# A routed product turned one unit ahead, with eight row buffers for its second part

## The chip, the cores and the metric

The kernel runs on one core of one Trainium2 chip. The metric is the device time of one execution in microseconds (us). Engine names are those of the profile: PE (TensorE matmuls), PEld (its weight loads), DVE (VectorE), ACT (ScalarE), POOL (GpSimd), SP (the queue that issues most DMAs).

## The reference

Input x is 64 sequences of 128 rows of 128, the context 64 x 120 rows. Four residual steps follow one another:

```
x = x + attention(layernorm(x) @ W0.T + b0, context, context)
x = x + shared_swiglu(n) + routed(n)             # n = layernorm(x)
x = x + attention(n Wq + bq, ctx Wk + bk, ctx Wv + bv)
x = x + trees(layernorm(x))                      # 8 decision trees of depth 7

def routed(x):                                   # 8 experts, H = 128, I = 256
    logits = x @ gate_w
    top_id, score = argmax(logits), sigmoid(max(logits))
    xs = x * score
    y = silu(xs @ rt_gate[e]) * (xs @ rt_up[e]) @ rt_down[e]   # e = top_id of the row
```

Each row goes through one expert only. The change touches the second step's routed part, and where the first steps of the second attention stand beside it.

## The kernel before, in words

Work is tiled by groups of G = 4 sequences (512 rows, NG = 16 groups). There are three stages in time.

*Phase A* (a_body, 19 rounds) computes the first attention, the shared expert and the logits of one group per round. Normalised rows are stored to rows2 in DRAM. DVE chooses each row's expert and its slot. POOL scales the rows by their score (scale) and scatters them with indirect DMAs, one per 128 rows, to x_sorted, a DRAM tensor in which every expert's rows fill whole tiles of 128 (scatter). This is done in two parts (halves) of 8 groups; the first part's 32 scatters lie in phase A, the second part's 32 follow it. The rows come back from rows2 into four buffers xs of one group each (load_rows, on SP); a buffer is loaded again when its four tiles have been scattered.

*The routed product* takes x_sorted in units of four tiles: 40 tiles a part, HR = 10 units, NR = 20 in both. For unit r SP loads it (r_load, two buffers xs_in), PE turns its tiles into PSUM bank 0 (r_turn), ACT copies them to xsT (r_evac_x), and PE multiplies them with the gate and up weights of each tile's expert, two tiles at a time, v = 0 and 1 (r_gate_up into banks 1, 2 and 3, 4). The weights were copied by DVE from WGU to w_now (r_weights), since the expert is known only at run time; experts_of reads it into registers. ACT takes silu (r_silu), DVE multiplies (r_mul), PE multiplies with the down weights (r_down, bank 6), and ACT copies the result to yo and stores it to y_sorted (r_evac_y). PE's order in r_body(r), line 1013: turn of unit r + 1, down of unit r - 1's second pair, first gate-up of unit r + 1, wait for the copy of y of unit r - 1, down of unit r's first pair, second gate-up of unit r + 1. All engines run in program order, so this order is set by hand. Units 1 to 8 are loops on PE and ACT, units 1 to 9 on DVE.

The second attention's steps for group 0, and some for group 1, are put by hand into late units, counted from FIRST_EARLY = HR + 2 = 12: c_rows3 (DVE adds routed rows and takes statistics), c_norm3, c_turn_x and c_scores (PE), c_xnT_evac and c_softmax (ACT), c_max_scores (DVE), c_turn_prob, c_pT_evac, c_values, c_rows4, c_norm4, c_turn_x4, c_x4_high, c_x4_low. DVE also splits the tree weights into a high and a low part there (split_trees_high, split_trees_low). POOL gathers the routed rows back by indirect DMA when the part's y is stored (gather).

*The trees* (phase_c, c_body) take one group per round of some 30 us; their first product is t_logits(0, 0), line 1125, behind a wait for the last copy of y at line 1123. The rest of the second attention runs inside these rounds.

The lines that matter: load_rows 441, SP's order after phase A 489 to 502, scale and scatter 530 to 546, POOL's order 572 to 576, ACT's r_body 730 to 755, PE's r_down 1004 and r_body 1013 to 1057, DVE's a_first_slots and a_pack (called at 1464 to 1468) and its units 1452 to 1498. These few lines set POOL's order for the second part:

```python
pool.wait_ge(scored, 2)
scale(HG)
pool.wait_ge(placed, 2)
for t in range(B0[1], B):
    scatter(t, 1, NG)        # calls scale(t // G + 1) at t % G == 2
```

## Time and profile before

| | |
|---|---|
| median of 3 runs | 853.05 us (853.01 to 855.39) |
| profiled execution | 849.45 us, its span 847.6 us |
| PE busy | 787.2 us, 93% of the span |
| PE weight loads | 633.5 us, 75% |
| DVE busy | 655.7 us, 77% |
| ACT busy | 541.6 us, 64% |
| POOL busy | 265.4 us, 31% |
| DMA | 55.88 MB, mean 66 GB/s |

The span runs from the first instruction to the last; the 1.8 us beside it lie around the program. Shares are means over stages that differ, so the rows below are read by stretch. In a timeline a number in brackets is the idle time of the engine before the instruction and, behind the arrow, what ended it; "issue" is time in which the profile shows no wait, and "remote" a release that it can't put to an instruction.

### The profile page before, as it was taken

To read this page: it belongs to the slowest core of one execution; us is meant where nothing else is said; L and a number is where in the kernel's file an instruction comes from. 1 tells how busy PE (TensorE), PEld (TensorE's weight loads), DVE (VectorE), ACT (ScalarE), POOL (GpSimd) and SP (SyncE) were. 2 spreads that over 40 slices of the span, in tenths; PEclk is the share of its full clock that TensorE was granted. 3 is DMA by queue.
4 is the path that set the end of the run, shared out by engine and by line. 5 is a ranking of instruction groups with operands and counts; after the bars stand their busy time and mean duration, and the time that the engine had idled before them with its cause. 6 is when DMAs were issued, how large, how long until landed. Compare 5 with 4: busy or idle time off the path is not lost.

```text
span 847.6 us, 15269 instructions
## 1 busy us (share of the span) xinstructions
PE 787.2 (93%) x4452; PEld 633.5 (75%) x4493; DVE 655.7 (77%) x1742; ACT 541.6 (64%) x948; POOL 265.4 (31%) x308
## 2 busy tenths in 40 slices
PE   5899998987878998999999999999999999999997
PEld 4788776776768898977777777777777777777775
DVE  5888889787844456768988887888888788888774
ACT  3577667565322334366877777777777777778765
POOL 2333222887287143112320321232132133111000
PEclk9999999999999999999999999999999999999999
DMA  6346784742334343100000000000000000000000
GB/s 170 89 137 191 194 221 130 202 130 85 87 108 149 95 116 91 51 26 13 26 23 4 25 25 0 25 25 19 6 25 25 0 25 25 11 14 14 14 1 25
DMA packets 91428, 55.88 MB, mean 66 GB/s; under 512 B 13439, under 2 KB 88055, under 8 KB 91255
## 3 DMA queue, kind: packets, MB, share of 16 engines
q1 hardware_dynamic: 75440, 41.29, 17.4%
q0 software_dynamic: 4096, 8.40, 3.5%
q10 hardware_dynamic: 11847, 5.64, 2.4%
q8 instruction: 23, 0.38, 0.2%
q14 instruction: 22, 0.18, 0.1%
HBM read 32.23 MB, written 23.07 MB: 65 GB/s over the span
## 4 chain that ended last, share of the span: by engine, by line
PE 41%; DVE 28%; issue 12%; ACT 12%; POOL 3%; another core or an unknown queue 2%; DVEq 1%; DMA 0%; ACTq 0%; POOLq 0%; SPq 0%
PE PS L823 7%; PE PS L808 6%; DVE sil_l L1522 4%; DVE dec L1506 3%; DVE xn_c L1149 3%; PE PS L1009 3%; PE PS L1068 3%; PE PS L1069 3%; PE PS L1070 3%; ACT sil L765 3%; DVE xn L1149 2%; PE PS L1090 2%; PE PS L1092 2%; PE PS L1091 2%; DVE st L1138 2%
## 5 line engine op out<-in xcount | busy, mean ns | idle before, releaser
L765 ACT ACTIVATE sil<-PS,b_in_c 128x512 f32<-128x512 f32 x256 | 162.3, 686 | 113.6 <-PE PS L1077 71.3
L1522 DVE TENSOR_TENSOR sil_l<-sil,sil_h 128x512 fp32r<-128x512 f32 x256 | 164.8, 685 | 44.7 <-ACT sil_h L773 44.3
L526 POOL TENSOR_TENSOR ve<-mv,eps 128x4 f32<-128x4 f32 x64 | 19.2, 300 | 450.2 <-DVE mv L1143 450.1
L773 ACT ACTIVATE sil_h<-sil 128x512 fp32r<-128x512 f32 x224 | 128.9, 631 | 0.0
L1090 PE MATMUL PS<-sil_h,wout_l 128*128 128x512 f32 x256 | 117.8, 460 | 1.6 <-DVE sil_l L1522 1.6
L1506 DVE TENSOR_SCALAR dec<-PS,b_in_c 128x512 bf16<-128x512 f32 x128 | 95.6, 747 | 26.1 <-PE PS L1070 24.3
L1068 PE MATMUL PS<-x4T_h,win_l 128*128 128x512 f32 x256 | 102.2, 399 | 1.6 <-ACT yo L725 0.7
L1092 PE MATMUL PS<-sil_h,wout_h 128*128 128x512 f32 x256 | 100.8, 394 | 0.0
L1091 PE MATMUL PS<-sil_l,wout_h 128*128 128x512 f32 x256 | 100.3, 392 | 0.0
L1069 PE MATMUL PS<-x4T_l,win_h 128*128 128x512 f32 x256 | 100.0, 390 | 0.0
L1070 PE MATMUL PS<-x4T_h,win_h 128*128 128x512 f32 x256 | 99.8, 390 | 0.0
L823 PE MATMUL PS<-xsT,w_now 128*128 128x128 f32 x640 | 81.4, 281 | 14.1 <-DVE ract L1442 6.9
L823 PEld LDWEIGHTS PS<-xsT,w_now 128*128 128x128 f32 x640 | 76.1, 195 | 16.3 <-issue 10.5
L584 POOL DMA_INDIRECT ys<-y_sorted,idx x64 | 69.8, 1090 | 28.1 <-issue 15.1
L528 POOL TENSOR_TENSOR rs<-ve,neg_half 128x4 f32<-128x4 f32 x64 | 70.6, 1103 | 5.0
L1090 PEld LDWEIGHTS PS<-sil_h,wout_l 128*128 128x128 f32 x256 | 48.3, 189 | 18.5 <-DVE sil_l L1522 6.4
L1209 DVE COPY w_now<-WGU 128x512 f32 x80 | 33.6, 461 | 36.7 <-PE PS L823 20.3
L1138 DVE BATCH_NORM_STATS2 st<-X 128x6 f32<-128x128 f32 (+1 forms) x256 | 55.5, 280 | 7.4 <-DMA X<-in_x 4.5
L1068 PEld LDWEIGHTS PS<-x4T_h,win_l 128*128 128x128 f32 x256 | 48.0, 188 | 17.3 <-issue 3.7
L1092 PEld LDWEIGHTS PS<-sil_h,wout_h 128*128 128x128 f32 x256 | 48.0, 188 | 11.2
L1070 PEld LDWEIGHTS PS<-x4T_h,win_h 128*128 128x128 f32 x256 | 48.0, 188 | 10.4
L1069 PEld LDWEIGHTS PS<-x4T_l,win_h 128*128 128x128 f32 x256 | 48.1, 188 | 9.4
(169 smaller groups left out, 1549.6 us busy)
## 6 DMA issues: line engine op xcount, KB each, us to landing
x_sorted<-zeros SPq DMA_DIRECT2D x4, 1280.0 KB, 6.8
xs_in<-x_sorted SPq DMA_DIRECT2D x20, 256.0 KB
y_sorted<-yo ACTq DMA_DIRECT2D x20, 256.0 KB
X<-in_x SPq DMA_DIRECT2D x16, 256.0 KB
rows<-xn SPq DMA_DIRECT2D x16, 256.0 KB
out<-res SPq DMA_DIRECT2D x16, 256.0 KB
ctxT<-in_ctx_t SPq DMA_DIRECT2D x16, 240.0 KB
ctx_rows<-in_ctx_kv SPq DMA_DIRECT2D x16, 240.0 KB
```

The lines of the kernel that those rows point to most:

```text
L765: act.activation(tile(sil[p % 2], c, W), bank(2 * (p % 2) + c), ACT.Silu, bias=b_in_c[:, 2 * p + c:2 * p + c + 1]).then_inc(t_silu, 1)
L773: act.activation(tile(sil_h[p % 2], c, W), tile(sil[p % 2], c, W), ACT.Copy).then_inc(t_hi, 1)
L823: i = pe.matmul(tile(bank(1 + 2 * v + t), n), tile(w_now[v], 2 * FC * t + n), tile(xsT[u], 2 * v + t), start=True, stop=True)
L1068: pe.matmul(dst, lo, x4T_h, start=True, stop=False, skip_group_check=True)
L1069: pe.matmul(dst, hi, x4T_l, start=False, stop=False, skip_group_check=True)
L1070: i = pe.matmul(dst, hi, x4T_h, start=False, stop=True, skip_group_check=True)
L1090: pe.matmul(bank(4), lo, act_h, start=(p == 0 and c == 0), stop=False)
L1091: pe.matmul(bank(4), hi, act_l, start=False, stop=False)
L1092: pe.matmul(bank(4), hi, act_h, start=False, stop=(p == TREES - 1 and c == 1)).then_inc(t_out, 1)
L1138: i = dve.bn_stats(st[:, s, j, :], cols(X, g * W + j * P, P))
L1506: dve.tensor_scalar(dec[p % 2], bank(2 * (p % 2)), b_in_c[:, 2 * p:2 * p + 1], 0.0, ALU.add, ALU.is_gt).then_inc(t_dec, 1)
L1522: dve.tensor_tensor(tile(sil_l[p % 2], c, W), tile(sil[p % 2], c, W), tile(sil_h[p % 2], c, W).bitcast(F32), ALU.subtract).then_inc(t_lo, 1)
```

## The change

- The turn of unit r + 2 is done in PE's r_body(r) after the first gate-up of unit r + 1; before, r_body(r) began with the turn of unit r + 1. Unit 1's turn moves into phase A.
- Row groups 12 to 15 get buffers of their own (late_rows, in the room of the shared expert's weights and rows), so the second part has eight. SP loads groups 10 to 15 at once after phase A, and no longer between units.
- POOL scales groups 8 to 11, all before the first scatter of the second part; ACT scales groups 12 to 15, four activations each, in units 1 to 4 between the copy of xsT and the second silu.
- Unit 9 and unit 19 have three tiles in place of four (39 tiles a part, since eight experts can leave at most seven partly filled tiles beside 32 full ones); y_sorted is one tile shorter.
- Steps of the second attention and the weight splits stand elsewhere in the late units; x4_low of group 0 and norm3, turn and copy of group 1 stand behind the last unit. ACT's loop over units is written out; DVE's loop ends at unit 7.
- The wait for the last copy of y stands behind the first tree product.

The diff, without the changed call signatures (r_weights, r_mul, r_silu and r_down take (r, v) for q) and the narrowing of their tiles to pair_tiles(r, v):

```diff
         xs = cut.two("xsa", W)
+        cut = Cut(TREE_W // 2, TREE_W)
+        late_rows = [cut.take(f"late_rows{i}", W) for i in range(XB)]
...
+        def rows_of(k):
+
+            return late_rows[k - HG - XB] if k >= HG + XB else xs[k % XB]
...
+        def near_end(r):
+
+            return isinstance(r, int) and r >= NR - 2
+
+        def pair_tiles(r, v):
+
+            return 1 if v and isinstance(r, int) and r in (HR - 1, NR - 1) else 2
+
+        def unit_tiles(r):
+
+            return 2 + pair_tiles(r, 1)
...
-                if i:
+                if k >= HG + XB:
+                    sp.wait_ge(a_g_ps, NG)
+                elif i:
                     sp.wait_ge(scattered[v], 16 * G * i)
                 sp.wait_ge(a_rows, 16 * (k + 1))
-                sp.dma_start(by_tile(xs[v]), rows2[k * G:(k + 1) * G, :, :].rearrange("b s d -> s b d")
-                             ).then_inc(k_in[v], 16)
+                sp.dma_start(by_tile(rows_of(k)), rows2[k * G:(k + 1) * G, :, :].rearrange("b s d -> s b d")
+                             ).then_inc(late_in[v] if k >= HG + XB else k_in[v], 16)
...
-            for k in range(HG + 2, HG + XB):
+            for k in range(HG + 2, NG):
                 load_rows(k)
             for r in range(HR - 2):
                 r_next(r, r % 2, 0)
-                if r > 2 and HG + XB + r - 3 < NG:
-                    load_rows(HG + XB + r - 3)
...
-                v = (t // G) % XB
-                if t % G == 2 and t // G + 1 < end:
-                    scale(t // G + 1)
-                pool.wait_ge(k_scaled, t // G + 1)
+                k = t // G
+                v = k % XB
+                if t % G == 2 and k + 1 < end:
+                    scale(k + 1)
+                if k < HG + XB:
+                    pool.wait_ge(k_scaled, k + 1)
+                else:
+                    pool.wait_ge(k_late, k - HG - XB + 1)
                 pool.sem_inc(pool_passed, 1)
                 pool.indirect_dma_start(x_sorted[h], bass.IndirectOffsetOnAxis(ap=POS[:, t:t + 1], axis=0),
-                                        tile(xs[v], t % G), None).then_inc(scattered[v], 16)
+                                        tile(rows_of(k), t % G), None).then_inc(scattered[v], 16)
...
-            scale(HG)
+            for k in range(HG, HG + XB):
+                scale(k)
             pool.wait_ge(placed, 2)
             for t in range(B0[1], B):
-                scatter(t, 1, NG)
+                scatter(t, 1, HG)
...
+            def scale(k):
+                act.wait_ge(late_in[k % XB], 16)
+                rows = rows_of(k)
+                for j in range(G):
+                    i = act.activation(tile(rows, j), tile(rows, j), ACT.Identity,
+                                       scale=SCORE[:, k * G + j:k * G + j + 1])
+                i.then_inc(k_late, 1)
...
-                r_silu(2 * r, 0)
-                if not last_unit(r):
+                r_silu(r, 0)
+                if r < NR - 1:
                     r_evac_x(r + 1, 1 - u)
-                if isinstance(r, int) and r == FIRST_EARLY + 3:
+                if 1 <= r <= XB:
+                    scale(HG + XB + r - 1)
+                if r == FIRST_EARLY + 3:
                     c_xnT_evac(0)
-                r_silu(2 * r + 1, 1)
-                if not first(r):
-                    r_evac_y(r - 1, 1 - u, stores, 1 if isinstance(r, int) and r > HR else 0)
-
-            r_body(0, 0, None)
-            with act.Fori(0, HR // 2 - 1) as i:
-                r_body(2 * i + 1, 1, i)
-                r_body(2 * i + 2, 0, i)
-            for r in range(HR - 1, NR):
+                if r == FIRST_EARLY + 4:
+                    c_softmax(0)
+                if r == FIRST_EARLY + 5:
+                    c_pT_evac(0)
+                if r == FIRST_EARLY + 7:
+                    c_x4_high(0)
+                r_silu(r, 1)
+                if r:
+                    r_evac_y(r - 1, 1 - u, stores, 1 if r > HR else 0)
+
+            for r in range(NR):
                 r_body(r, r % 2, (r - 1) // 2)
-                if r == FIRST_EARLY + 3:
-                    c_softmax(0)
-                if r == FIRST_EARLY + 4:
-                    c_pT_evac(0)
-                if r == FIRST_EARLY + 6:
-                    c_x4_high(0)
-                if r == FIRST_EARLY + 7:
-                    c_xnT_evac(1)
             r_evac_y(NR - 1, 1, NR // 2 - 1, 1)
+            c_xnT_evac(1)
...
                     r_gate_up(0, 0, 0, 0)
+                    r_turn(1, 1)
...
@@ -1016,25 +1044,24 @@
                 q = 2 * r
                 if not end:
                     coming = experts_of(pe, r + 1)
-                    r_turn(r + 1, 1 - u)
                 if not first(r):
-                    r_down(q - 1, 1, was)
+                    r_down(r - 1, 1, was)
                 if not end:
                     r_gate_up(q + 2, 0, r + 1, 1 - u)
+                    if not near_end(r):
+                        r_turn(r + 2, u)
                 if now is None:
                     now = experts_of(pe, r)
                 if isinstance(r, int):
                     if r == FIRST_EARLY + 3:
                         c_scores(0)
-                    if r == FIRST_EARLY + 4:
-                        c_turn_prob(0)
-                    if r == FIRST_EARLY + 6:
+                    if r == FIRST_EARLY + 5:
+                        c_values(0)
+                    if r == FIRST_EARLY + 7:
                         c_turn_x4(0)
-                    if r == FIRST_EARLY + 7:
-                        c_turn_x(1)
                 if not first(r):
                     pe.wait_ge(r_y, r)
-                r_down(q, 0, now)
+                r_down(r, 0, now)
                 if end:
                     return now
                 r_gate_up(q + 3, 1, r + 1, 1 - u)
...
                 if r == FIRST_EARLY + 2:
                     c_turn_x(0)
                 if r == FIRST_EARLY + 4:
-                    c_values(0)
+                    c_turn_prob(0)
             now = r_body(NR - 1, 1, now, coming, end=True)
-            r_down(2 * NR - 1, 1, now)
+            r_down(NR - 1, 1, now)
+            c_turn_x(1)
...
-            pe.wait_ge(r_y, NR)
             pe.wait_ge(tree_split, 2)
             t_logits(0, 0)
+            pe.wait_ge(r_y, NR)
             phase_c(pe, c_body)
...
-            with dve.Fori(1, HR) as r:
+            with dve.Fori(1, HR - 2) as r:
                 coming = r_first(r)
                 r_second(r, coming)
-            for r in range(HR, NR - 1):
+            for r in range(HR - 2, NR - 1):
                 coming = r_first(r)
                 if r == FIRST_EARLY + 1:
                     c_rows3(0)
-                if r == FIRST_EARLY + 3:
-                    c_max_scores(0)
-                if r == FIRST_EARLY + 5:
-                    c_rows4(0)
+                if r == FIRST_EARLY + 2:
+                    c_norm3(0)
                 if r == FIRST_EARLY + 6:
-                    c_rows3(1)
+                    c_norm4(0)
                 r_second(r, coming)
                 if r == HR + 1:
                     split_trees_high()
+                if r == FIRST_EARLY:
+                    split_trees_low(win_l, win_f, win_h)
                 if r == FIRST_EARLY + 2:
-                    c_norm3(0)
-                if r == FIRST_EARLY + 1:
-                    split_trees_low(win_l, win_f, win_h)
+                    split_trees_low(wout_l, wout_f, wout_h)
+                if r == FIRST_EARLY + 3:
+                    c_max_scores(0)
                 if r == FIRST_EARLY + 4:
-                    split_trees_low(wout_l, wout_f, wout_h)
+                    c_rows3(1)
                 if r == FIRST_EARLY + 5:
-                    c_norm4(0)
-                if r == FIRST_EARLY + 6:
-                    c_x4_low(0)
-                    c_norm3(1)
-            r_mul(2 * NR - 2, 0)
-            r_mul(2 * NR - 1, 1)
+                    c_rows4(0)
+            r_mul(NR - 1, 0)
+            r_mul(NR - 1, 1)
+            c_x4_low(0)
+            c_norm3(1)
```

## Rows read from the trace of the kernel before

**Rows 1.** The page's first line: span and number of instructions.
```profile
span 847.6 us, 15269 instructions
```

**Rows 2.** Stretches (start:end, length): busy us (x instructions) by engine, clock, DMA.
```profile
225.95:241.95 16.00, 11.54 (x98) 10.90 (x97) 12.05 (x26) 3.86 (x7) 9.33 (x10) 1.00 0.25 74
241.95:282.09 40.14, 31.91 (x262) 29.84 (x261) 15.88 (x29) 11.30 (x20) 29.61 (x30) 1.00 0.44 135
282.09:317.61 35.52, 35.52 (x313) 35.22 (x313) 19.59 (x40) 13.04 (x24) 9.35 (x10) 1.00 0.37 102
317.61:330.60 12.99, 12.35 (x110) 12.16 (x109) 10.59 (x26) 4.35 (x8) 7.86 (x8) 1.00 0.36 105
330.60:365.83 35.23, 31.74 (x263) 30.99 (x261) 22.57 (x59) 15.72 (x26) 2.91 (x4) 0.95 0.19 54
365.83:847.60 481.77, 469.53 (x2232) 353.50 (x2272) 395.53 (x929) 356.97 (x585) 108.69 (x123) 1.00 0.06 17
294.18:300.04 5.86, 5.86 (x55) 5.86 (x53) 2.90 (x6) 2.17 (x4) 0.00 (x0) 1.00 0.31 89
```

**Rows 3.** Timeline of PE in body 9: turn, down, gate-up, down.
```profile
294.18 0.60 PE L808 MATMUL PS<-WA,xs_in 128*128 128x128 f32 x4
294.62 1.06 PE L1009 MATMUL PS<-WD,ract 128*128 x8
295.51 2.01 PE L823 MATMUL PS<-xsT,w_now 128*128 128x128 f32 x16
297.36 1.06 PE L1009 MATMUL PS<-WD,ract 128*128 x8
```

**Rows 4.** Timelines of DVE, POOL and PE where the second part is placed.
```profile
213.79 0.20 DVE L1380 TENSOR_TENSOR expert_f<-expert_f,c_rout 128x40 f32<-128x40 f32 x1
...
223.95 0.94 DVE L1357 CAST tiles_f<-tiles_i 128x8 f32<-128x8 int32 x1
...
232.42 1.72 DVE L1380 TENSOR_TENSOR expert_f<-expert_f,c_rout 128x40 f32<-128x40 f32 x1
...
223.83 1.04 POOL L534 TENSOR_TENSOR xsa<-xsa,SCORE 128x512 f32<-128x512 f32 x1 [9.51 <-ACT SCORE L633]
...
237.38 2.05 PE L823 MATMUL PS<-xsT,w_now 128*128 128x128 f32 x16 [2.53 <-DVE ract L1442]
```

**Rows 5.** Timelines in bodies 3 and 4: late copies, and what waits for them.
```profile
249.31 0.66 PE L808 MATMUL PS<-WA,xs_in 128*128 128x128 f32 x4
...
252.64 0.60 ACT L629 ACTIVATE xsT<-PS 128x512 f32<-128x512 f32 x1 [5.03 <-remote]
...
253.46 2.05 PE L823 MATMUL PS<-xsT,w_now 128*128 128x128 f32 x16 [2.60 <-issue]
...
261.13 2.05 PE L823 MATMUL PS<-xsT,w_now 128*128 128x128 f32 x16 [1.61 <-ACT xsT L629]
...
263.31 0.69 DVE L1442 TENSOR_TENSOR ract<-sg,PS 128x512 f32<-128x512 f32 x1 [2.64 <-remote]
...
264.02 1.15 PE L1009 MATMUL PS<-WD,ract 128*128 x8 [0.85 <-issue]
```

**Rows 6.** Timeline of POOL: first and last of the second part's 32 scatters.
```profile
230.72 1.01 POOL L545 DMA_INDIRECT x_sorted<-xsa,POS  x1 [5.86 <-DVE POS L1370]
...
279.07 0.96 POOL L545 DMA_INDIRECT x_sorted<-xsb,POS  x1 [0.30 <-issue]
```

**Rows 7.** Body 15: DVE's maximum, PE's next gate-up, and the stretch behind.
```profile
334.87 0.66 DVE L1403 TENSOR_REDUCE nmax<-PS 128x4 f32<-128x480 f32 x1 [3.48 <-PE PS L977]
...
337.63 3.51 PE L823 MATMUL PS<-xsT,w_now 128*128 128x128 f32 x16 [1.90 <-DVE ract L1442]
...
338.00:342.00 4.00, 4.00 (x23) 4.00 (x23) 1.44 (x4) 0.99 (x3) 0.00 (x0) 0.59 0.00 0
```

**Rows 8.** The last unit: DVE's norm3 of group 1, PE's first tree product.
```profile
359.97 1.11 DVE L1149 TENSOR_SCALAR xn_c<-X,mv,rs 128x128 f32<-128x128 f32 x4
...
365.83 0.50 PE L1068 MATMUL PS<-x4T_h,win_l 128*128 128x512 f32 x1 [0.69 <-ACT yo L725]
```

More of the change, by code:

```diff
@@ L85, in program @@
     x_sorted = [nc.dram_tensor(f"x_sorted{h}", (HTILES[h] * P, P), F32, kind="Internal").ap() for h in range(HALVES)]
-    y_sorted = [nc.dram_tensor(f"y_sorted{h}", (HTILES[h] * P, P), F32, kind="Internal").ap() for h in range(HALVES)]
+    y_sorted = [nc.dram_tensor(f"y_sorted{h}", ((HTILES[h] - 1) * P, P), F32, kind="Internal").ap() for h in range(HALVES)]
     rows2 = nc.dram_tensor("rows2", (B, P, P), F32, kind="Internal").ap()
@@ L324, in last @@
             return isinstance(g, int) and g >= NG - n
-        def last_unit(r):
-            return isinstance(r, int) and r == NR - 1
+        def near_end(r):
[4 more added lines that the diff above has]
+            return 2 + pair_tiles(r, 1)
         DVE_TREE = 1
@@ L714, in c_x4_high, with r_silu @@
                 act.activation(x4T_h, bank(7), ACT.Copy).then_inc(c_x4h, 1)
[L717 to L720 removed]
+            def r_silu(r, v):
+                n = pair_tiles(r, v)
+                act.wait_ge(r_gu_ps, 2 * r + v + 1)
+                pair = by_tile(PS[:, 512 * (1 + 2 * v):512 * (1 + 2 * v + n)], 512)
+                act.activation(by_tile(sg[v][:, 0:n * FI], FI), pair[:, :, 0:FI], ACT.Silu).then_inc(r_sg, 1)
             def r_evac_y(r, u, stores, h):
@@ L820, in r_gate_up @@
                     pe.wait_ge(r_act, q - 1)
-                for t in range(2):
+                for t in range(pair_tiles(r, v)):
                     for n in range(2 * FC):
@@ L1002, in _, with r_down @@
             pe.wait_ge(a_rows, 16 * NG)
-            def r_down(q, v, experts):
-                pe.wait_ge(r_act, q + 1)
-                for t in range(2):
+            def r_down(r, v, experts):
+                pe.wait_ge(r_act, 2 * r + v + 1)
+                for t in range(pair_tiles(r, v)):
                     for c in range(FC):
@@ L1202, in take_logits, with r_weights @@
                 dve.tensor_tensor(dst, dst, src[:, :, 0:n, E:2 * E], ALU.add).then_inc(a_lg, 1)
-            def r_weights(q, v, experts):
-                if not below(q, 2):
-                    dve.wait_ge(r_gu_ps, q - 1)
-                for t in range(2):
+            def r_weights(r, v, experts):
+                if not below(r, 1):
+                    dve.wait_ge(r_gu_ps, 2 * r + v - 1)
+                for t in range(pair_tiles(r, v)):
                     i = dve.tensor_copy(tile(w_now[v], t, 2 * FI),
@@ L1241, in a_body @@
                     a_choose(4)
[L1242 removed]
+                    r_weights(0, 1, experts_of(dve, 0))
                 if route == "pack":
```

41 lines of the change are left out of this document (20 added, 21 removed).

## The prediction

> **What bounds the kernel now.** I read the span first [rows 1], then busy time by stretches cut at the starts of units [rows 2], and inside those stretches each engine's timeline for what ended its idle time. "Body r" is PE's r_body(r); it starts with the turn of unit r+1. The kernel has three stages: phase A up to 226 us, the routed product from 226 to 366 us, and the trees from 365.83 us to the end. The change works on the second. The trees take 481.8 us, PE busy in 469.5 of them [rows 2]; nothing in their loop is edited, so I carry that stretch over unchanged.
>
> An undisturbed body is PE-bound: 5.86 us with PE busy for all of it, DVE for 2.90 and ACT for 2.17 [rows 2]. It is turn 0.44, down 0.89, gate-up 1.85, down 0.89 (starts 294.18, 294.62, 295.51, 297.36 [rows 3]), and the remaining 5.86 - 4.07 = 1.79 is the second gate-up. Against 5.86 each, the stretches of rows 2 overrun as follows:
> - bodies 0 and 1: 16.00 - 11.72 = 4.3 us
> - bodies 2 to 6: 40.14 - 29.30 = 10.8 us; this is where the second part's scatters run [rows 6]
> - bodies 7 to 12: 35.52 - 35.16 = 0.4 us
> - bodies 13 and 14: 12.99 - 11.72 - 0.44 (attention's turn) = 0.8 us
> - body 15 to the first tree product: 35.23 us, worked out below
>
> So the stage has some 20 us that isn't PE work. The question is which of it the change reaches.
>
> **Part 1, the end of the stage (moved attention steps, tile 39 of unit 19, tree logits ahead of the last wait).** Before, DVE takes attention's row maximum in the middle of body 15, idle 3.48 us until the scores are there; the weights of the next gate-up queue behind it, and PE idles 1.90 us [rows 7]. The gate-up after that takes 3.51 us instead of 1.85. After the change the maximum stands behind DVE's second half, which is done when silu is; DVE's 1.3 us of maximum and shift then end before body 15 does, and the weights (0.76 us) are ready 0.9 us into body 16. ScalarE's exp with its two table loads (1.28 us each) stands in ScalarE's body 16 ahead of silu, whose product PE wants only a body later. I find no new PE wait in bodies 15 to 18. The tightest place is the first weights copy of DVE's unit 18, behind attended rows and statistics: on my schedule it ends 0.1 us before PE wants it.
>
> PE's sum from body 15: body 15 with scores (eight matmuls, as a down, 0.89) 6.75; body 16 5.86; turn of prob 0.44; body 17 with values 6.75; body 18 without a turn and with a one-tile second gate-up 5.86 - 0.44 - 0.90 = 4.52; then down 0.89, attention's turn 0.44, downs 0.89 + 0.45, turn 0.44. That is 27.4. The tail gains waits: turn, x4 high on ScalarE (0.60, the length of the evacuation in rows 5), silu, y's evacuation, then the last downs; and on DVE product, x4 low and norm3 (1.11 [rows 8]) before the last turn. I put these at 1.6 + 0.3 = 1.9 us. Total 29.3 against 35.2: **5.9 us saved**. Today's tail also idles 0.69 us before the first tree product, for the last y [rows 8]; that wait moves behind the product.
>
> **Part 2, bodies 13 and 14.** DVE's routed rows and statistics (some 2.2 us) and the 2.3 us split of win no longer fall into one body. DVE's own 2.9 us plus 2.3 fits in 5.86. **0.8 us saved.**
>
> **Part 3, 39 tiles in unit 9.** One tile less of gate-up (half of 1.79) and of down (half of 0.89) in a PE-bound body: **1.3 us saved.** Turning still does four tiles.
>
> **Part 4, the turn a unit ahead, in bodies 2 to 6.** Here I see a lag that I can't explain. The turn at 249.31 should be over by 250, yet ScalarE's copy of it starts at 252.64, and PE's next gate-up at 253.46, 2.60 us idle. The same form gives 1.61 us at 261.13 [rows 5] and a third, smaller one 0.6, 4.8 us together. In the new order the turn is followed by attention steps, down, a gate-up and the next body's down before its result is needed: 0.89 + 1.79 + 0.89 = 3.6 us, less 0.6 of copying, is 3.0 us of cover against 0.3 now. That covers all three. A second lag, from a down to y's evacuation and the next down, cost 0.85 at 264.02 [rows 5] and 0.2 at 270.9; its cover grows by the turn's 0.44, so 0.6 back. **5.4 us saved**, if it is a lag of the signal. If the array itself stands still, looking ahead gives back nothing; these are my two ends, 0 and 5.4, and I take 5.4, because PE's records run on during the lag: it starts the gate-up at 261.13 while the down before it is signalled only at 263.3, when DVE's product that waits for it starts [rows 5]. The Trainium skill, page "SBUF — State Buffer", section "SBUF: two separate sides", says that DMA traffic can't slow an engine's SBUF access; that speaks for a lag over a stalled array, and the trace, where DMA is busiest just there, can't yet tell.
>
> **Part 5, scaling and buffers.** POOL scatters 32 tiles from 230.72 to 280.0 [rows 6], with seven scales between. A scale is 1.05 us and a scatter has a pitch of 1.27, so without scales 32 x 1.27 = 40.6 us: the end comes near 272. Nothing that sets the end waits for it: load 10 was free to start at 282 and its turn came at 294. Moving it early costs at the front. Scales 9, 10 and 11 now run back to back behind scale 8 at 223.83, next to DVE's routing chain, which is what holds PE to 237.38 (2.53 idle) [rows 4]. The 0.17 us cast L1357 took 0.94 beside scale 8, and L1380 took 1.72 beside the scale that stands at 233.0 against 0.20 alone [rows 4]. So the chain loses up to 3 x 1.05 = 3.2 us, and gains 1.5 from the scale that leaves its place there; bounds -1.5 and +3.2. Most of the chain's steps are much shorter than the POOL work around them, so I take +1.5, which gives a sum of **0**. The Trainium skill, page "SBUF — State Buffer", section "Who interferes with whom", calls this an exclusive lock, held for a whole instruction; L1357 and L1380 agree. By that rule alone each added scale can hold the chain once, the upper bound.
>
> ScalarE's four scales (four 128x128 each; between 0.6 us, one 128x512 [rows 5], and 2.4, four such) fall in bodies 1 to 4, where ScalarE is idle 3.7 us of 5.86 and about 2 of it at that place. I take 1.0 and cost it at nothing. SP's four more row loads (1 MB) go ahead of load 2, which then lands 3 to 5 us later, still before its turn near 229.7.
>
> **Sum.** 5.9 + 0.8 + 1.3 + 5.4 + 0 = 13.4 us. The profiled execution took 849.45 us (span 847.6 and 1.8 around it), so 836.0 for one profiled like it; the median of the runs shown is 3.6 us above it, and 853.05 - 13.4 = **839.6 us**.
>
> **Rivals.**
> - *The lag stays (0.25).* PE really stands still in bodies 2 to 6, and the scatters are as many as before. Only 8.0 us come back: 845.0. For it: the overrun is only where scatters run. Against: PE's records run on.
> - *The lag goes altogether (0.12).* It comes from rows, scales and scatters together; rows and scales leave. 10.8 instead of 5.4 us back: 834.2.
> - *DVE's chain gets longer (0.12).* Each of the three scales holds it once: +3.2, without the gain: 842.8.
> - *PE's clock (0.05).* After today's 1.90 us idle PE ran 338 to 342 at a granted clock of 0.59, which is the level of 1.2 GHz for most of it; the gate-up at 337.63 took 3.51 us [rows 7]. The new tail has a 1.6 us idle of its own, so the fall may come back at the first trees: 1.7 us lost, 841.3.
> - *It does nothing measurable (0.05).* That needs the end of the stage to be refilled by DVE: rows 4 ahead of unit 18's weights late by several us. About 852.
> - *Slower (0.04).* ScalarE stands in order: its wait for late row group 12 is ahead of unit 1's second silu, near 237 us. The load leaves SP near 218. Each us beyond 237 delays all engines; the change is slower from a landing at about 251 us on, and at 256 costs 5 us net: 858. Against it: the DMA engines are a quarter busy from 226 on [rows 2].
>
> **How the numbers follow.** The forecast has 0.37. The range takes in the four cases from 834.2 to 845.0 with about 1 us for the spread of runs: 833.5 to 847. A measurement here tells 0.3% (2.6 us) from no change. Faster: the forecast and the first four rivals, 0.91, less some doubt on steps I haven't seen: 0.89. Same 0.06, slower 0.05.
>
> **What would show it.** Part 1: PE without a wait above 0.5 us from the start of body 15 to the last unit, no fall of its clock near 338, and 29 us to the first tree product. Part 4: copies of the turn may still start late, but no gate-up idles for them; wrong if bodies 2 to 6 still sum to 40 us. Part 5: last scatter near 272; unit 2's first gate-up starts within 1.5 us of 237.4. The trees must again take 482 us. The prediction fails if ScalarE or DVE waits in bodies 1 to 4 for rows, or if the overrun in bodies 2 to 6 doesn't move.

## The result, and the profile after

The change made the kernel slower on the chip of its first measurement: a median of 862.64 us (861.47 to 862.72) against 853.03 us, a ratio of 1.0124 with a 95% interval of 1.0084 to 1.0164. The prediction was 839.6 us, with a range of 833.5 to 847.0: wrong in sign. On another chip, below, the same two kernels come out at a ratio of 0.993, some 6 us saved, where the forecast's sum without Part 4 is 8.0.

The profiled execution after has a span of 859.7 us [rows 1: 847.6]. Its stretches, cut where those of [rows 2] are (start of body 2, of body 7, of body 15, first tree product); the first start is worked out, 238.58 of unit 2's gate-up below plus 1.85 + 0.44 + 0.89 + 1.79; columns as in [rows 2]:

```profile
span 859.7 us, 15178 instructions
243.55:300.91 57.36, 38.45 (x284) 36.99 (x285) 17.42 (x36) 16.95 (x37) 22.99 (x24) 0.79 0.28 83
300.91:347.37 46.46, 46.46 (x416) 46.46 (x417) 31.55 (x65) 17.81 (x32) 17.51 (x17) 1.00 0.37 107
347.37:377.89 30.52, 27.68 (x246) 27.29 (x245) 19.48 (x56) 14.01 (x24) 2.47 (x4) 1.00 0.19 53
377.89:859.70 481.81, 470.14 (x2235) 353.30 (x2273) 395.52 (x929) 357.87 (x587) 108.56 (x123) 1.00 0.06 17
```

Where the 12.06 us (377.89 - 365.83) went:

| stretch | before | after | difference |
|---|---|---|---|
| start of body 2 (after has one turn more ahead of it, 0.4) | 241.95 | 243.55 | +1.6 |
| bodies 2 to 6 | 40.14 | 57.36 | +17.2 |
| bodies 7 to 14 | 48.51 | 46.46 | -2.05 |
| body 15 to the first tree product | 35.23 | 30.52 | -4.7 |
| trees | 481.77 | 481.81 | 0 |

So the later stretches did about what was forecast, and one stretch, bodies 2 to 6, lost more than all of it. PE there, body 1 to body 2 and again in body 3:

```profile
235.84 1.95 PE L850 MATMUL PS<-xsT,w_now 128*128 128x128 f32 x16
237.62 1.12 PE L1037 MATMUL PS<-WD,ract 128*128 x8
238.58 1.95 PE L850 MATMUL PS<-xsT,w_now 128*128 128x128 f32 x16
240.36 0.27 PE L835 MATMUL PS<-WA,xs_in 128*128 128x128 f32 x1
241.53 0.38 PE L835 MATMUL PS<-WA,xs_in 128*128 128x128 f32 x2 [0.89 <-issue]
...
258.59 2.07 PE L1037 MATMUL PS<-WD,ract 128*128 x8 [15.29 <-issue]
...
273.20 0.48 PE L850 MATMUL PS<-xsT,w_now 128*128 128x128 f32 x2 [0.45 <-issue]
274.61 0.50 PE L850 MATMUL PS<-xsT,w_now 128*128 128x128 f32 x3 [0.93 <-issue]
```

PE's records stop for 15.29 us. Just before this hole, and again from 273 us on, its groups of four and sixteen matmuls come broken into ones, twos and threes with idle time between them. Behind the hole the matmuls run at half their speed (2.07 us for a down that takes 1.06): the granted clock is 0.50, the level of 1.2 GHz, from 246 to 262 us. The signals for the same matmuls, in ACT and DVE:

```profile
235.23 1.26 ACT L651 ACTIVATE late_rows<-late_rows,SCORE 128x128 f32<-128x128 f32 x4
247.24 0.60 ACT L749 ACTIVATE sg<-PS 128x512 f32<-128x512 f32 x1 [10.74 <-remote]
257.80 0.60 ACT L755 ACTIVATE yo<-PS 128x512 f32<-128x512 f32 x1 [9.96 <-remote]
...
261.47 0.60 ACT L749 ACTIVATE sg<-PS 128x512 f32<-128x512 f32 x1 [3.08 <-remote]
...
247.46 0.94 DVE L1237 COPY w_now<-WGU 128x512 f32 x2 [9.61 <-remote]
```

The silu at 247.24 wants the gate-up recorded at 235.84, and the copy of y at 257.80 the down recorded at 237.62: 9.5 and 19 us after their ends (237.79 and 238.74). The silu at 261.47 wants the gate-up recorded at 238.58, 21 us after its end (240.53). So what PE's records call done is signalled far later. This trace doesn't tell whether the work itself or only its signal was late; a_gather below says something on it. The record of 258.59 stands behind such a signal: PE's program waits there for the copy of y, 257.80 + 0.60 = 258.40, and that copy waits for PE's own down. POOL beside it, 20 scatters without a pause from 232.93 on, and then:

```profile
257.10 0.96 POOL L564 DMA_INDIRECT x_sorted<-late_rows,POS  x1 [0.30 <-issue]
264.52 0.96 POOL L564 DMA_INDIRECT x_sorted<-late_rows,POS  x1 [6.46 <-ACT late_rows L651]
...
280.69 0.96 POOL L564 DMA_INDIRECT x_sorted<-late_rows,POS  x1 [6.25 <-ACT late_rows L651]
```

The signal that lets PE go on comes at 257.80, inside the last scatter of POOL's burst (257.10 to 258.06), and not before. POOL stops only because ScalarE's next scale, in ScalarE's order behind copies and silus that wait for PE, hasn't been done. Then POOL starts the next burst, of eight, at 264.52, and PE is slowed in it again: from unit 4's turn (266.01) to unit 6's (285.61) it takes 19.6 us for two bodies. The scatters end at 285.65, not near 272.

### The profile page after: what moved, and what is told of

The parts are those of the page before. It is cut to its first block, busy times and chain, and to the rows that moved or that the text cites. A ratio compares the mean times of both kernels' runs of the same rounds, so it can differ in the third digit from the quotient of the medians.

```text
span 859.7 us, 15178 instructions
## 1 busy us (share of the span) xinstructions
PE 789.1 (92%) x4436; PEld 636.0 (74%) x4477; DVE 653.4 (76%) x1740; ACT 546.5 (64%) x964; POOL 259.5 (30%) x304
## 3 DMA queue, kind: packets, MB, share of 16 engines
q1 hardware_dynamic: 75440, 41.29, 17.2%
## 4 chain that ended last, share of the span: by engine, by line
PE 45%; DVE 27%; issue 14%; ACT 10%; POOL 3%; DVEq 1%; another core or an unknown queue 1%; DMA 0%; ACTq 0%; POOLq 0%; SPq 0%
PE PS L850 8%; PE PS L835 6%; PE PS L1037 4%; DVE sil_l L1551 4%; DVE dec L1535 3%; DVE xn_c L1177 3%; PE PS L1096 3%; PE PS L1098 3%; PE PS L1097 3%; ACT sil L792 3%; PE PS L1118 2%; DVE xn L1177 2%; PE PS L1120 2%; PE PS L1119 2%; PE PS L858 2%
## 5 line engine op out<-in xcount | busy, mean ns | idle before, releaser
L850 PEld LDWEIGHTS PS<-xsT,w_now 128*128 128x128 f32 x632 | 78.5, 202 | 8.5 <-issue 7.8
L604 POOL DMA_INDIRECT ys<-y_sorted,idx x64 | 71.9, 1123 | 27.9 <-issue 15.1
L749 ACT ACTIVATE sg<-PS 128x512 f32<-128x512 f32 (+1 forms) x40 | 23.5, 586 | 76.6 <-PE PS L850 60.2
L1237 DVE COPY w_now<-WGU 128x512 f32 x78 | 30.6, 432 | 48.3 <-PE PS L850 28.4
L1037 PE MATMUL PS<-WD,ract 128*128 x312 | 44.5, 288 | 18.0 <-issue 15.3
```

The source lines that it names most:

```text
L850: i = pe.matmul(tile(bank(1 + 2 * v + t), n), tile(w_now[v], 2 * FC * t + n), tile(xsT[u], 2 * v + t), start=True, stop=True)
L1037: i = pe.matmul(tile(bank(6), 2 * v + t), tile(ract[v], FC * t + c), cols(WD, experts[2 * v + t] * (FC * P) + c * P, P), start=(c == 0), s ...
```

## The experiments

The theory (theory 1 in what was expected): POOL's indirect DMAs, issued without a pause, hold PE's array or its signals; before, POOL's scale after every fourth scatter let PE go, and the change took these scales away. Rivals: the hold comes from the scatters' writes and the DMA traffic; from PE's register reads of the experts; from the new PE order; or from the row loads that SP issues at once, with POOL's pauses having no part. The yardstick is the time from unit 3's turn to unit 8's, five bodies (T3 to T8): 29.3 us by the undisturbed body of [rows 3], 40.14 before and 57.2 after. Kernels of one chip share their runs of the kernel before.

### Chip 8 (before 847.76 us)

**a_poolscale**: the change, with POOL scaling every group between scatters, as before.

```diff
-                if k < HG + XB:
-                    pool.wait_ge(k_scaled, k + 1)
-                else:
-                    pool.wait_ge(k_late, k - HG - XB + 1)
+                pool.wait_ge(k_scaled, k + 1)
...
-            for k in range(HG, HG + XB):
-                scale(k)
+            scale(HG)
             pool.wait_ge(placed, 2)
             for t in range(B0[1], B):
-                scatter(t, 1, HG)
+                scatter(t, 1, NG)
...
-                if 1 <= r <= XB:
-                    scale(HG + XB + r - 1)
```

> The changed kernel with one part undone: POOL scales all groups itself, one scale of 1.05 us after every fourth scatter, as before; ScalarE's four scales and POOL's three scales ahead of the first scatter go; eight buffers and all else stay. Theory 1 (PE stands still while POOL issues scatters without a pause; each pause lets it go on): the 15.3 us gap of PE goes, the bodies from unit 2's first gate-up to body 7 take about 45 us again in place of 62, and the time falls by 17 to 20 us, to about 844. Rival 2 (the new order on PE, with the turn behind the gate-up, makes the stall): it stays, about 861. Rival 3 (the four more row loads at 218 us make it): it stays too, and so would a gap in a kernel that only has those.

Measured: 843.1 us, ratio 0.9927 (0.9897 to 0.9958); T3 to T8 34.07 us. One part undone, and there is a gain of 0.7% where the first chip had a loss of 1.2%; the change as it is wasn't run on chip 8, but a_gather and a_static below, which differ from it elsewhere, take 860.84 and 858.89 us here. What is left of the hold shows its form. POOL's scales, ACT's and DVE's first work after them:

```profile
251.10 1.05 POOL L552 TENSOR_TENSOR late_rows<-late_rows,SCORE 128x512 f32<-128x512 f32 x1
257.22 1.05 POOL L552 TENSOR_TENSOR late_rows<-late_rows,SCORE 128x512 f32<-128x512 f32 x1
263.47 1.05 POOL L552 TENSOR_TENSOR late_rows<-late_rows,SCORE 128x512 f32<-128x512 f32 x1
...
251.23 0.60 ACT L748 ACTIVATE sg<-PS 128x512 f32<-128x512 f32 x1 [4.07 <-remote]
258.12 0.60 ACT L748 ACTIVATE sg<-PS 128x512 f32<-128x512 f32 x1 [3.92 <-remote]
264.36 0.60 ACT L748 ACTIVATE sg<-PS 128x512 f32<-128x512 f32 x1 [3.63 <-remote]
...
279.49 0.69 DVE L1468 TENSOR_TENSOR ract<-sg,PS 128x512 f32<-128x512 f32 x1 [4.78 <-remote]
```

Each late signal comes within or at the end of a scale; the last burst has six scatters (270.93 to 278.27) and no scale behind it, and there the signal comes 1.2 us after its end. That last burst costs more behind the yardstick: from unit 8's turn (273.09) to unit 9's (283.57) it takes 10.48 us, 4.7 above a body of 5.80. The theory holds; PE's new order and SP's row loads are still in this kernel, so these two rivals fall as causes of the large hold.

**b_eight**: the kernel before, with the eight buffers and the new scaling alone.

```diff
-            scale(HG)
+            for k in range(HG, HG + XB):
+                scale(k)
             pool.wait_ge(placed, 2)
             for t in range(B0[1], B):
-                scatter(t, 1, NG)
+                scatter(t, 1, HG)
...
+                if isinstance(r, int) and 1 <= r <= XB:
+                    scale(HG + XB + r - 1)      # on ScalarE
```

> The kernel before with one part of the change alone: eight row buffers, groups 8 to 11 scaled by POOL ahead of the first scatter, groups 12 to 15 by ScalarE in units 1 to 4 (its loop over units written out for that), and all row loads after phase A. PE's order, the attention steps and 40 tiles stay. Theory 1 (scatters without a pause): PE gets a gap of 10 us and more here too, the time rises by 15 to 20 us, to about 870. Rival 2 (PE's new order): the time stays within 2 us of before, or 3 above it for DVE's chain beside POOL's scales.

Measured: 866.53 us, ratio 1.0201 (1.0157 to 1.0244). The one part alone makes the loss, in PE's old order too. Its two holes lie ahead of unit 3's turn (262.62), so the yardstick misses them: T3 to T8 is 37.2 us, and unit 2's turn to unit 8's 62.9 us, against 48.8 in the kernel before on the first chip.

```profile
245.50 3.64 PE L841 MATMUL PS<-xsT,w_now 128*128 128x128 f32 x16 [7.10 <-issue]
257.41 2.07 PE L1027 MATMUL PS<-WD,ract 128*128 x8 [8.27 <-ACT yo L745]
```

**a_gather**: the change, with the second part's indirect DMAs reading from x_sorted into the row buffers in place of writing, so that part's rows don't reach x_sorted.

```diff
-                pool.indirect_dma_start(x_sorted[h], bass.IndirectOffsetOnAxis(ap=POS[:, t:t + 1], axis=0),
-                                        tile(rows_of(k), t % G), None)
+                pool.indirect_dma_start(tile(rows_of(k), t % G), None, x_sorted[h],
+                                        bass.IndirectOffsetOnAxis(ap=POS[:, t:t + 1], axis=0))
```

> The changed kernel with the second part's 32 scatters turned round: the same 32 indirect DMAs of 128 rows at the same places of POOL's program, but from x_sorted to the row buffers. The second part of the routed product is thus computed from zeros and its result isn't the reference's. If POOL's issuing of indirect DMAs without pause holds PE, the gap of about 15 us stays. If it is the direction, rows read from SBUF and written to DRAM, PE has no gap above 2 us in bodies 1 to 6, and the time is near 842.

Measured, one execution: 860.84 us, T3 to T8 55.9 us. The direction doesn't matter. Two silus of this run say something on the signals:

```profile
262.70 0.60 ACT L753 ACTIVATE sg<-PS 128x512 f32<-128x512 f32 x1 [15.57 <-remote]
...
264.84 0.59 ACT L753 ACTIVATE sg<-PS 128x512 f32<-128x512 f32 x1
```

The first wants the gate-up recorded from 239.46 to 241.51. Between that gate-up and the next silu's, PE does a turn, a down and a gate-up, 28 matmuls: 3.1 us at 0.11 us each, and some 6 us at the granted clock of 0.50 here. The two silus are 2.14 us apart. So PE had done part of the 28 before the first silu started: the signal came later than the work.

**a_static**: the change, with PE using experts 0 to 3 for every unit's down product in place of the ones it reads.

```diff
+            if eng is nc.tensor:
+                return [0, 1, 2, 3]
             word = eng.value_load(
```

> The changed kernel, but PE reads no expert numbers from SBUF and always takes the down weights of experts 0 to 3 (its result isn't the reference's); matmuls, waits and signals are as many. If PE's own register reads, or addresses that are known only at run time, are what waits behind POOL's scatters, the gap goes and the time is near 842. If the array or PE's signals are held, the gap of about 15 us stays, and the time is within 2 us of the changed kernel.

Measured, one execution: 858.89 us, T3 to T8 54.8 us. The rival of the register reads falls. And in this kernel the hold is seen matmul by matmul:

```profile
247.32 0.37 PE L852 MATMUL PS<-xsT,w_now 128*128 128x128 f32 x1 [1.16 <-issue]
248.01 0.37 PE L852 MATMUL PS<-xsT,w_now 128*128 128x128 f32 x1 [0.33 <-issue]
...
255.73 0.37 PE L1039 MATMUL PS<-WD,ract 128*128 128x128 f32 x1 [1.51 <-issue]
256.43 0.37 PE L1039 MATMUL PS<-WD,ract 128*128 128x128 f32 x1 [0.33 <-issue]
257.13 0.58 PE L1039 MATMUL PS<-WD,ract 128*128 128x128 f32 x1 [0.33 <-issue]
259.93 0.37 PE L1039 MATMUL PS<-WD,ract 128*128 128x128 f32 x1 [2.22 <-issue]
```

Starts are 0.70 us apart, or 1.4, 2.1 and 2.8; at full speed they are 0.11 apart (16 in 1.79). At most one or two matmuls start in 0.70 us until 262.03, 3.2 us after POOL's burst ended (257.86 + 0.96 = 258.82; its next scatter is at 264.64). So the array or what feeds it is slowed as well, and not only a signal late.

### Chip 1 (before 840.02 us)

**a_half**: the change, with POOL scaling two tiles after every second scatter (all groups on POOL).

```diff
+                if h and t % G == 2 and k + 1 < end:
+                    scale_half(k + 1, 0)
+                if h and t % G == 0 and k > HG:
+                    scale_half(k, 1)
```

> The changed kernel, but POOL scales all groups of the second part itself, two tiles (128x256, some 0.55 us) after every two scatters, so that no more than two scatters follow each other without a pause, except the last four; eight buffers and PE's new order stay. Theory 1 (PE slows down more the longer POOL issues scatters without a pause; from the third or fourth on it all but stands): bodies 1 to 6 lose nearly nothing, PE's stretch from unit 2's first gate-up to body 7 is near 38 us, the time 4 to 6 us below the one with pauses after every four, about 838. Rival (each scatter costs PE a fixed time, whatever stands between): as with pauses after every four, about 843.

Measured: 838.98 us, ratio 0.9987 (0.9978 to 0.9997); T3 to T8 29.7 us.

**a_land4**: the change, with POOL waiting after every fourth scatter until the four have landed.

```diff
                                         tile(rows_of(k), t % G), None).then_inc(scattered[v], 16)
+                if h and t % G == G - 1:
+                    pool.wait_ge(scattered[v], 16 * G * (k // XB + 1))
```

> The changed kernel with one wait added: after each fourth scatter of the second part POOL waits until the four have landed, and does no other work in the pause. Scaling stays as the change has it. If only POOL's pause matters, whatever fills it, PE's 15 us gap goes and the time is near 845. If the scales themselves (an operation that holds DVE's port) are what lets PE go on, the gap stays, near 860.

Measured, one execution: 846.65 us; T3 to T8 29.8 us.

**a_pooldma** and **a_spdma**: the change, with the second part's rows stored by plain DMAs in row order in place of by expert (so x_sorted's second part holds other rows), issued by POOL and by SP.

```diff
-                pool.indirect_dma_start(x_sorted[h], ..., tile(rows_of(k), t % G), None)
+                pool.dma_start(x_sorted[h][(t - B0[1]) * P:(t - B0[1] + 1) * P, :], tile(rows_of(k), t % G))
```

> The changed kernel with the second part's 32 scatters as plain DMAs of the same 128 rows from POOL, to rows in order, no list of addresses (the routed result isn't the reference's). If any DMA whose descriptors POOL writes holds PE, the gap stays, about 860. If it is the indirect form alone, the gap goes, about 842.

> The changed kernel with the second part's 32 scatters as plain DMAs issued by SP, four after each load of a unit (the routed result isn't the reference's); POOL issues nothing there, the bytes and descriptors moved are the same. If POOL's writing of descriptors holds PE, PE has no gap above 1 us in bodies 1 to 7 beyond the front, and the time is 835 to 840. If the DMA traffic itself holds PE, gaps of several us remain.

Measured, one execution each: 833.08 and 833.71 us, neither with a hold.

But nothing was held on this chip in any of the four, and before itself took 840 us, not 848 to 853. So these four say nothing on the hold yet. They do show a limit that the hold had covered. In a_half the scatters end at 280.06, and in a_land4 near 288; unit 10's load wants them all, and PE arrives at it earlier now:

```profile
285.15 1.11 PE L848 MATMUL PS<-WA,xs_in 128*128 128x128 f32 x4 [4.69 <-DMA xs_in<-x_sorted]
...
292.77 1.11 PE L837 MATMUL PS<-WA,xs_in 128*128 128x128 f32 x4 [10.57 <-DMA xs_in<-x_sorted]
```

### Chip 9 (before 840.47 us): is it the chip?

**before2** and **after2** are the two kernels unchanged, **a_poolscale2** and **a_half2** repeat a_poolscale and a_half.

> The kernel before, unchanged, to have its profile from the chip of this series, since its time was 853, 848 and 840 us in three series. If chips differ in how much POOL's scatters hold PE, bodies 2 to 6 take another time here than the 40.1 us of the first profile (29.3 if not held at all), and phase A and the trees take the same. If chips differ otherwise, these move too.

> The changed kernel, unchanged, beside the others on one chip. It should again have a gap on PE behind the fifth or so of the scatters without a pause; on a chip where the kernel before is at 840 us, the ratio to before is then above the 1.012 of the first series if the long burst holds PE everywhere, and below it if such a chip hardly knows the hold.

> Scales on POOL after every fourth scatter, all else as changed: again 0.7% below before (0.990 to 0.996). On a chip with little hold it gains only what doesn't hang on scatters, some 8 us of the sum, 1%, if load 10 doesn't come late.

> Half scales on POOL after every second scatter: PE isn't held in bodies 2 to 6 (cadence 5.8 to 6.1 us), but PE waits for load 10, since the last scatter is issued only near 280 us; between 0.990 and 1.000 of before, the same as with pauses after every four within 2 us.

Measured: before2 841.04 us (one execution), after2 834.1, ratio **0.993** (0.9908 to 0.9953), a_poolscale2 835.42, ratio 0.9942 (0.9921 to 0.9964), a_half2 839.03, ratio 0.9988 (0.9974 to 1.0002). Bodies 2 to 6 of before2 and of after2 (here to the worked-out end of body 6; body 7's down starts at 273.04):

```profile
244.05:274.62 30.57, 30.54 (x263) 29.39 (x261) 15.35 (x30) 10.86 (x20) 25.07 (x26) 1.00 0.55 162
...
242.81:272.72 29.91, 29.50 (x262) 29.10 (x260) 14.95 (x30) 13.71 (x28) 22.90 (x24) 1.00 0.44 130
```

The same kernels, with more bytes per us than on the first chip (162 GB/s against 135 in [rows 2]), and no hold in either; after2 was expected to have one. The hold goes with the chip. But the runs of one chip were made together and no numbered chip was visited twice, so nothing tells the chip from something else that may have changed with it. Here the change is faster, and its scaling part is worth something: after2's scatters end at 274.1 and unit 10's turn, at 281.61, waits for nothing, while a_poolscale2 waits 0.79 us and a_half2 4.94 us there.

### Chip 6 (before 853.28 us)

**a_pooldma2** and **a_land4b** repeat a_pooldma and a_land4.

> The changed kernel with plain DMAs from POOL for the second part's 32 scatters (routed result isn't the reference's), once more, since the first time the kernel before was at 840 us and such a chip hardly knows the hold. If this series has the kernel before at 847 us or more: the gap of 10 us and more on PE stays if any DMA from POOL makes it, about 860; it goes, about 840, if it needs the indirect form. With before at 840 us it tells nothing new: about 833.

> The changed kernel with POOL waiting after each fourth scatter until the four have landed, once more. With before at 847 us or more: PE is held 1 to 2 us in each burst of four as in the kernel before, and then waits some 5 to 10 us for load 10, about 850, if a pause in which POOL does nothing is as good as one with a scale; a gap of 10 us inside the scatters if it isn't. With before at 840 us: about 846, the wait for load 10 alone.

Measured, one execution each: a_pooldma2 834.46 us, T3 to T8 29.8 us: no hold from 32 plain DMAs with as many bytes on the same queue, the first 24 of them back to back from 234.10 to 247.41. That this chip does hold is seen in a_mix below. So the rival of the traffic falls; it takes the indirect kind. Their issue is shorter too, eight in 4.57 us, and a long issue by itself can't be told from the indirect kind by this. a_land4b took 845.56 us, T3 to T8 33.1 us, then 4.49 us for unit 10's load; against 57.2 in the change as it is. Its pauses are idle:

```profile
234.10 4.57 POOL L565 DMA_DIRECT2D x_sorted<-xsa  x8 [4.05 <-DVE POS L1402]
...
239.86 0.96 POOL L564 DMA_INDIRECT x_sorted<-xsa,POS  x1 [2.11 <-DMA x_sorted<-xsa,POS]
246.71 0.96 POOL L564 DMA_INDIRECT x_sorted<-xsb,POS  x1 [2.10 <-DMA x_sorted<-xsa,POS]
```

The first line is a_pooldma2, the others a_land4b. ScalarE's scales and the front are here as in the change, so the pause is what frees PE, whether POOL computes in it or not. In this pause the four DMAs also land; a pause with DMAs in flight was tried only with a scale in it.

**a_mix**: the change, with groups 9 to 11 scaled by POOL between scatters, and a memset of 128x32 ahead of every second one of the last sixteen.

```diff
-                if t % G == 2 and k + 1 < end:
+                if t % G == 2 and k + 1 < min(end, HG + XB):
                     scale(k + 1)
+                if h and t % G in (0, 2) and k >= HG + XB:
+                    pool.memset(tile(pad, (t - (HG + XB) * G) // 2, 32), 0.0)
```

> The changed kernel with scales 9, 10 and 11 back on POOL between scatters, and for groups 12 to 15, which ScalarE scales, a memset of 128x32 on POOL ahead of every second scatter as a pause. With before at 840 us: as fast as the change without its longer front, 1 to 2 us below it, 0.990 to 0.993 of before. With before at 847 us or more: if a pause of some 0.3 us is enough, 0.985 to 0.990; if it must be as long as a scale, PE gets gaps of several us in the last 16 scatters, 1.00 to 1.01.

Measured: 857.49 us, ratio 1.0054 (1.0029 to 1.008); T3 to T8 53.2 us. The memset fits into the 0.30 us between two scatters, their pitch doesn't grow, and PE's records have a hole of 14.59 us where the scales end; the copy of y that ends it starts at 272.11, 3.1 us after the burst's last scatter (268.97). A scale of 1.05 us is enough of a pause, a memset of 0.14 to 0.28 us inside the gap is not.

## Why the prediction was wrong, step by step

**Part 4, the overrun of bodies 2 to 6: the step that failed.** I saw the 10.8 us, saw that they lay only where scatters ran, gave a stalled array a chance of 0.25, and then let that case cost nothing more than a saving missed. My two ends were 0 and 5.4 us saved. The lower end was not an end: with a stalled array, the change edits what stalls it. "The scatters are as many as before" was true, and the pauses between them, which Part 5 took away, were what bounded the hold. The measured value is -17.2 us, where +5.4 was forecast. By the runs, b_eight and a_poolscale, the scaling part alone accounts for the loss. The argument for a lag ("PE's records run on") was half the matter: signals do come late, by up to 21 us after the records, but the matmuls are slowed too (0.70 us and more between starts in a_static), and both come from the same bursts, which looking ahead doesn't shorten. The trace before had a sign that the length of a burst counts, and I didn't use it. Its last six scatters, 272.69 to 280.03, have no scale among or behind them, and at their end a gate-up comes broken into eleven, four and one, with 1.9 us idle:

```profile
277.88 1.39 PE L823 MATMUL PS<-xsT,w_now 128*128 128x128 f32 x11
279.88 0.62 PE L823 MATMUL PS<-xsT,w_now 128*128 128x128 f32 x4 [0.61 <-issue]
281.31 0.27 PE L823 MATMUL PS<-xsT,w_now 128*128 128x128 f32 x1 [0.81 <-issue]
282.09 0.65 PE L808 MATMUL PS<-WA,xs_in 128*128 128x128 f32 x4 [0.51 <-issue]
```

The sentence of the Trainium skill, page "SBUF — State Buffer", section "SBUF: two separate sides", on DMA traffic that I set against it didn't decide the matter either: plain traffic holds nothing (a_pooldma2), as it says. The Trainium skill says in that section, of the SBUF ports, that PE and ACT "never wait on anyone". PE does wait beside POOL's indirect DMAs here, and no run shows whether it is at a port; whoever reads the sentence as "nothing on POOL can slow PE" is set right by the measurement. Whether looking ahead gives anything where nothing is held: on chip 9 bodies 2 to 6 took 30.57 us before, so there was at most 1.3 to win. Whether it gives anything where PE is held isn't shown: no pair of runs on one such chip differs in PE's order alone.

**Part 5, the front.** Three added scales held DVE's chain once each:

```profile
223.79 0.93 DVE L1385 CAST tiles_f<-tiles_i 128x8 f32<-128x8 int32 x1
224.76 0.97 DVE L1386 TENSOR_TENSOR_SCAN tile_end<-c_rout,tiles_f 128x8 f32<-128x8 f32 x1
225.76 0.96 DVE L1387 TENSOR_TENSOR first_slot<-tile_end,tiles_f 128x8 f32<-128x8 f32 x1
226.75 0.97 DVE L1388 TENSOR_SCALAR first_slot<-first_slot 128x8 f32<-128x8 f32 x1
...
234.63 0.20 DVE L1408 TENSOR_TENSOR expert_f<-expert_f,c_rout 128x40 f32<-128x40 f32 x1
```

The first took 0.94 already [rows 4]; the next three are short steps stretched to a scale's length, 0.8 us each, and the fifth gives back 1.5 (1.72 in [rows 4]). That is +0.9 for the sum of 0 that I took, and unit 2's first gate-up starts at 238.58, 1.2 later than 237.38. I argued from short chain steps beside long POOL work; the point is that a short step too is held until the scale ends, and four scales back to back catch four steps. The rule of an exclusive lock in the Trainium skill, page "SBUF — State Buffer", section "Who interferes with whom", gave the upper end, and the count of held steps agrees with it. ScalarE's scales took 1.26 us, not 1.0. That these scales should stand behind work that waits for PE, and so set POOL's pace through PE's own delay, was in no step; it is what closes the loop at 258 and 274 us.

**"Nothing that sets the end waits for the scatters."** True for PE's old pace, with unit 10's turn at 294 [rows 3]. In after2 that turn is at 281.61, and the scatters' end at 274.1 is then needed (a_half2 waits 4.94 us for an end at 280).

**Part 3, 39 tiles: mis-sized.** I took half a gate-up and half a down, 1.3 us. Only the down is narrower:

```profile
310.82 1.95 PE L850 MATMUL PS<-xsT,w_now 128*128 128x128 f32 x16
...
318.40 0.61 PE L1037 MATMUL PS<-WD,ract 128*128 x4
```

The second down of unit 9, at 318.40, has four matmuls. Its second gate-up, at 310.82, still has sixteen, since body 8 issues it inside PE's loop, where the unit is a register and pair_tiles gives 2. The body takes 5.35 instead of 5.80: 0.45 us.

**Part 2 and bodies 7 to 14.** 2.05 us came back against 2.1 forecast (parts 2 and 3), but from other places: 0.45 from the tile, 8 x 0.06 = 0.5 because an undisturbed body is 5.80 and not 5.86 (the first gate-up 1.79 instead of 1.85, no longer right behind its turn), and 1.1 from overruns that are gone. Before had 48.51 - 8 x 5.86 - 0.44 = 1.2 of overrun there, after has 46.46 - 8 x 5.80 - 0.44 + 0.45 = 0.1. A sum that comes out right doesn't show that its terms do.

**Part 1, the end of the stage: right, 4.7 of 5.9 us.** The clock didn't fall; 347 to 378 runs at 1.00 where [rows 2] had 0.95.

```profile
367.79 0.76 DVE L1237 COPY w_now<-WGU 128x512 f32 x2 [0.54 <-issue]
368.47 0.68 DVE L1471 TENSOR_TENSOR ract<-sg,PS 128x512 f32<-128x512 f32 x1
...
369.29 2.02 PE L850 MATMUL PS<-xsT,w_now 128*128 128x128 f32 x16 [1.25 <-DVE ract L1471]
376.02 1.64 PE L1037 MATMUL PS<-WD,ract 128*128 x12 [1.59 <-ACT yo L755]
```

The missing 1.2 us is one wait, 1.25 us at 369.29, above the 0.5 us that I had set as the most. It is at the place I had called the tightest, DVE's unit 18 behind attended rows and statistics; I had put the weights 0.1 us ahead of PE's need, and what PE waits for is the product after them. The tail's wait of 1.59 is the 1.6 of the sum. On chip 9 the same stretches took 30.50 and 35.16 us: 4.7 again.

**The whole, where nothing is held.** On chip 9 the trees start 7.4 us earlier (357.44 to 350.00): front 1.2, bodies 2 to 6 0.3, bodies 7 to 14 1.2, end 4.7. Parts 1 to 3 as forecast were 8.0. The rival "the lag stays", 845.0 from 853.05, had just this size; it is right about a chip that the prediction wasn't made for. None of my cases had a change of the hold itself, so the chance of slower, 0.05, hung on one mechanism (a late row group, which didn't happen) instead of on the unexplained 10.8 us.

**Which version to keep.** a_poolscale beats the kernel before where PE is held (0.9927 on chip 8), and by the first chip's loss the change too, though the two never ran side by side there. It is within 0.2% of the change where it isn't (835.42 and 834.1 on chip 9). It keeps PE's new order, the eight buffers and the moved steps, and only leaves scaling where it was.

## What to carry to other kernels

An overrun that you can't explain has no lower bound at zero: ask which of the change's edits touch its suspected cause, in either direction, before costing them. Removing work from an engine off the critical path also removes the pauses in what it issues; when a stream of POOL's indirect DMAs runs beside PE-bound work, keep bursts to about four with a pause of 1 to 2 us, and don't leave a longer one at the end. And look at who receives PE's results as well as at PE's records: a result can be signalled up to 21 us after its record ends.

## What the runs showed of the hardware

- While POOL issues indirect DMAs back to back (pitch 1.27 us), PE can be held: down to one 128x128 matmul in 0.70 us or more (a_static), its signals up to 21 us behind its records, up to 15.29 us between two records; scatters and gathers alike. The hold can outlast the last issue of a burst by some 3 us (a_static 3.2, a_mix 3.1). Plain DMAs of POOL (0.55 us each) don't do it.
- A pause of about 1 us of other POOL work, or 2.1 us of idleness, mostly frees it. In bodies 2 to 6, bursts of four with a scale between cost the kernel before 10.8 us on the first chip; in the new order they cost 4.8 (34.07 - 29.3) on chip 8, and the last six scatters 4.7 more in body 7; with an idle pause 3.8 (33.07 - 29.3) on chip 6; and a burst of twenty, then of eight, 28 (57.36 - 29.3) on the first chip. Since the chips differ, these costs compare only roughly.
- It goes with the chip, or with something else that changed with the chip: PE is held on the first, 8 and 6 (before 853.05, 847.76 and 853.28 us), and not on 1 and 9 (840.02 and 840.47). For the kernel before, the difference lies in bodies 2 to 6: 40.14 - 30.57 = 9.6 us there, 847.6 - 839.2 = 8.4 between the spans.
- What sets the chips apart and what within the indirect kind holds PE was not tried and stays open. The later gathers don't show it: bodies 7 to 14 overrun by 0.1 us with twelve gathers beside them. These come in fours with 1 us or more between (322.85 to 328.71, then from 329.76), which fits the pauses but isn't a test of them.
